# Cross-attention in float32 on one core: the products with the values in batch 6 issued as two runs of two head groups instead of four runs of one

## What is computed

```python
Q = (query @ Wq.T + bq); K = (key_value @ Wk.T + bk); V = (key_value @ Wv.T + bv)
scores = jnp.einsum('bhqd,bhkd->bhqk', Q, K) / np.sqrt(D_K)
attn = jax.nn.softmax(scores, axis=-1)
context = jnp.einsum('bhqk,bhkd->bhqd', attn, V)
output = context @ W_o.T + b_o
x = output + query
return (x - mean(x)) / sqrt(var(x) + 1e-5) * ln_gamma + ln_beta
```

## Time and profile before

| what | before |
|---|---|
| median of 3 runs | 141.59 us (141.34 to 142.11) |
| the profiled execution's own time | 142.33 us |
| its span, first to last instruction | 140.4 us |
| PE busy | 130.2 us, 93% of the span |
| DVE busy | 96.9 us, 69% |
| ACT busy | 88.2 us, 63% |
| POOL busy | 82.2 us, 59% |
| granted TensorE clock, mean | 0.999 |

### The profile page before, as it was taken

One profiled execution on the slowest core, in us unless ns is written; L12 is line 12 of the kernel. 1 busy time (PEld: TensorE's weight loads), 2 busy tenths in 40 slices (PEclk: granted clock), 3 DMA queues, 4 the chain that ended last, 5 costly groups with the idle time before them and its releaser, 6 DMA issues.

```text
span 140.4 us, 3935 instructions
## 1 busy us (share of the span) xinstructions
PE 130.2 (93%) x1481; PEld 115.1 (82%) x1481; DVE 96.9 (69%) x226; ACT 88.2 (63%) x179; POOL 82.2 (59%) x105
## 2 busy tenths in 40 slices
PE   4999989799999999998999999999999999999960
PEld 4899966689788979897999998998989888877730
DVE  5977799888837875678559756975687788521442
ACT  3468544458485847668585859574958556788510
POOL 8357899993722853205079975860489106589181
PEclk9999999999999999999999999999999999999999
DMA  4996797882279832651226025642280000011102
GB/s 98 351 363 231 208 295 226 304 254 108 61 185 298 244 131 69 217 173 55 72 105 229 5 72 170 230 163 60 75 298 3 24 20 5 4 37 35 37 0 65
DMA packets 16067, 19.59 MB, mean 139 GB/s; under 512 B 2592, under 2 KB 15456, under 8 KB 16048
## 3 DMA queue, kind: packets, MB, share of 16 engines
q1 hardware_dynamic: 14944, 17.42, 38.5%
q0 software_dynamic: 640, 1.64, 4.4%
q10 hardware_dynamic: 464, 0.28, 0.7%
HBM read 6.30 MB, written 0.92 MB: 51 GB/s over the span
## 4 chain that ended last, share of the span: by engine, by line
PE 84%; DVE 6%; DMA 5%; issue 1%; ACTq 1%; POOLq 0%; SPq 0%; ACT 0%; DVEq 0%
PE m_bank L885 19%; PE pv_bank L991 14%; PE mx_bank L940 14%; PE st_bank L973 14%; PE m_bank L1022 4%; PE st_bank L885 3%; DMA q_stack<-shift_half 3%; DVE mx L742 3%; PE mx_bank L1071 3%; PE m_bank L1002 2%; PE m_bank L913 2%; PE mx_bank L973 2%; DMA q_stack<-shift 2%; PE m_bank L1010 1%; ACTq L277 1%
## 5 line engine op out<-in xcount | busy, mean ns | idle before, releaser
L742 DVE TENSOR_REDUCE mx<-mx_bank 112x1 f32<-112x375 f32 x128 | 63.8, 540 | 21.8 <-PE mx_bank L940 21.5
L628 ACT ACTIVATE pw<-st_bank 125x448 f32<-125x448 f32 x86 | 45.3, 544 | 19.4 <-PE st_bank L973 18.9
L940 PE MATMUL mx_bank<-k_stack,q_stack 128*112 128x376 f32 x128 | 43.2, 352 | 0.1
L973 PE MATMUL st_bank<-q_stack,k_stack 128*125 128x224 f32 x172 | 34.8, 284 | 1.8 <-DMA q_stack<-shift_half 1.3
L973 PEld LDWEIGHTS st_bank<-q_stack,k_stack 128*125 128x125 f32 x172 | 28.6, 186 | 5.2 <-issue 2.7
L940 PEld LDWEIGHTS mx_bank<-k_stack,q_stack 128*112 128x112 f32 x128 | 22.0, 176 | 2.9 <-issue 1.5
L431 POOL TENSOR_TENSOR k_hl<-k_full,k_hl 128x376 fp32r<-128x376 f32 x10 | 10.3, 1032 | 19.8 <-ACT k_hl L549 19.8
L991 PE MATMUL pv_bank<-pw,v_sb 125*17 125x112 f32 x744 | 21.5, 260 | 0.0
L991 PEld LDWEIGHTS pv_bank<-pw,v_sb 125*17 125x17 f32 x744 | 16.7, 97 | 3.1 <-issue 1.9
L885 PE MATMUL m_bank<-w_hl,c_hl 128*125 128x256 f32 x126 | 18.1, 282 | 0.0
L405 POOL TENSOR_TENSOR c_hl<-c_raw,c_hl 128x752 fp32r<-128x752 f32 x6 | 11.2, 1861 | 10.6 <-ACT c_hl L520 10.6
(11 more groups left out here) (115 smaller groups left out, 177.4 us busy)
## 6 DMA issues: line engine op xcount, KB each, us to landing
k_stack<-k_hl SPq DMA_DIRECT2D x48, 188.0 KB, 2.7
c_raw<-ctxT SPq DMA_DIRECT2D x8, 375.0 KB, 3.9
q_stack<-q_hl SPq DMA_DIRECT2D x9, 112.0 KB, 2.3
x_space<-x_nat SPq DMA_DIRECT2D x4, 224.0 KB, 3.1
out<-yo SPq DMA_DIRECT2D x8, 112.0 KB, 2.0
pw<-wT SPq DMA_DIRECT2D x2, 256.0 KB, 4.7
q_stack<-q_hl POOLq DMA_DIRECT2D x3, 168.0 KB, 2.8
q_stack<-q_hl SPq DMA_DIRECT2D x3, 168.0 KB, 2.9
```

The costliest lines, as they stand in the source:

```text
L628: nc.scalar.activation(p_tile[0:KC, n % PR, :, :], st_of(n)[0:KC, 0:4 * Q].rearrange("p (j q) -> p j q", j=4), ACT.Exp, scale=float(DK) ** ...
L742: nc.vector.tensor_reduce(mx[b % 2][:, h % 2, q_pair(h // 2):q_pair(h // 2) + 1], mx_bank[n % MR][0:Q, 0:KV], axis=AX_X, op=ALU.max, negat ...
L940: nc.tensor.matmul(mx_bank[n % MR][0:Q, 0:KVP], q_stack[k][:, side, q_pair(h // 2), b - Q_STACKS[k][0], :], k_stack[b % 3][:, h // 2, :], ...
L973: last = nc.tensor.matmul(st_of(n)[0:KC, k * 2 * Q:(k + 1) * 2 * Q], k_stack[i % 3][:, 2 * g + k, c * KC:(c + 1) * KC], q_stack[qk][:, :, ...
```

## The change

One constant is different, so that the rule for runs of two groups holds for batch 6 too, up to unit 86:

```diff
         WIDE = UNITS * (B - 2) + 4
         LATE = WIDE + 2
-        SINGLE = UNITS * (B - 2) + NC
+        SINGLE = UNITS * (B - 1) + NC
         wide_ring = st_bank + mx_bank[0:2]
```

## The result

| | before | after |
|---|---|---|
| median of 20 runs each | 141.55 us (141.27 to 142.69) | 142.28 us (141.79 to 143.01) |
| the profiled execution's own time | 142.33 us | 141.97 us |
| its span | 140.4 us | 140.2 us |
| granted TensorE clock, mean | 0.999 | 0.998 |

The ratio is 1.0041, with a 95% interval of 1.0026 to 1.0056: by the ratio the change makes the kernel slower by 0.58 us, with an interval of 0.37 to 0.79 (the medians as they stand in the table are 0.73 apart). The forecast was +0.60.

What follows compares the result with a forecast made beforehand. TensorE (PE), busy 93% of the span, was taken as the bound. Last group's end -0.28, then +0.95 to the copy in place of 0.07, gives +0.60 us: 141.59 + 0.60 = 142.2 us, range 141.5 to 142.8.

Steps and rivals of the forecast that it cites:

- The saving: On PE, merging two runs into others saves 0.33 us each, -0.66 us in all.
- Step 1: Unit 77's pair, no longer covered by group 0's run, waits for unit 75's exponential to free its bank: +0.26 us.
- step 2: PE's projection (0.86), transposes and units 78 and 79, then run one without a wait, ending at 121.56 us.
- Step 3: Unit 84's pair, fifth behind run one, waits for unit 80's exponential to free its bank: +0.33 us.
- the ring: Four banks used in turn by score pairs; unit 84's pair therefore needs unit 80's exponential to end.
- Step 4: Unit 84 also waits for the maxima's DMA, landing about 122.4 us, ahead of the exponential's 122.56: no cost, margin 0.15.
- Step 5: Projection, unit 85's pair, then run two without a wait, ending at 125.50 us; PE 0.28 us ahead of before.
- Step 6: Unit 86's pair follows run two; its exponential precedes the copy of the sums on ACT, ending the copy 0.60 us later.
- Step 7: PE finishes units 87 and 88, stands until the copy; transposes begin 0.60 us later, the whole tail moving with them.
- saving and waits cancel: Rival: the two bank waits cost nothing, the copy is back at 126.39 and nothing moves; 141.6 us, chance 0.15.
- the saving reaches the end: Rival: the full 0.66 us comes through if the copy does not hold the transposes; 141.0 us, chance 0.08.

Runs made afterwards that it cites:

- experiment 8: Changed kernel with unit 86's pair ahead of the second run, batch 5's projection ahead of unit 84, batch 4's ahead of unit 77 (its input copied earlier): ratio 0.9934.
- Experiment 3: Changed kernel with the output projection of batch 5 ahead of unit 84's score pair instead of behind it: ratio 1.0019, stretch 9.40 us.
- experiment 6: Changed kernel with the transpose of batch 7's maxima ahead of the output projection of batch 4: ratio 1.0066, stretch 10.04 us.
- Experiment 4: Kernel before with only the second run merged (groups 2 and 3 behind unit 85): ratio 1.0068; profiled a second time for its stretch, 10.18 us.
- Experiment 1: Changed kernel with unit 86's score pair back ahead of the second run: ratio 1.0001, stretch 9.11 us.
- experiment 2: Changed kernel with ACT's copy of batch 6's sums behind unit 85's exponential instead of unit 86's: ratio 0.9962, stretch 8.88 us.
- experiment 5: Only the first run merged (groups 0 and 1 behind unit 79), groups 2 and 3 apart as in the kernel before: ratio 1.0019, stretch 9.18 us.
- experiment 7: Changed kernel with unit 86's pair ahead of the second run and batch 5's projection ahead of unit 84: ratio 0.9969, stretch 8.81 us.

## Why the prediction was right, step by step

- **The saving, 0.66 us.** Right in size: experiment 8, in which neither bank wait is left and the copy isn't late, has 0.63. It was not enough to foretell the sign. The Trainium skill (TensorEngine Tiling (Array Packing), Key Properties) states that a change of tiling mode drains the array. The trace agrees, with the 0.63.
- **Step 1, the wait at unit 77, 0.26.** Measured 0.25. Missing from the step is the projection behind it, 0.08 longer than the 0.86 of step 2.
- **Step 3, the wait at unit 84, 0.33.** Measured 0.31. Experiment 3 takes it away by cover alone, experiment 6 shows that the ring holds it even with an early DMA.
- **Step 4, the DMA of the maxima, margin 0.15.** The step was wrong in its sum, without an effect on the result. L955 ends at 120.48, where its next piece begins; I had added its 0.10 once more. By the step's own sum it should come 0.64 us earlier, not 0.74. Measured it came 0.57 earlier, the projection's 0.08 being the rest (the first issue is at 119.38 - 116.71 = 2.67 from the transposes of batch 5, before at 120.81 - 117.57 = 3.24), and the margin was nothing: landing and exponential fell on the same 121.75. Experiment 4 shows what lies behind: 0.71 us of idle weight loads, named DMA.
- **Step 5, the second run 0.28 ahead of where the last group had ended.** Counted from L1002 of batch 5 it ends at 124.69 - 116.71 = 7.98, and the last group before at 125.78 - 117.57 = 8.21: 0.23 ahead. The difference is the 0.08, less 0.03 by which the two waits were shorter.
- **Step 6, the copy behind the exponential of unit 86, 0.60 later.** The copy begins at 125.58 - 116.71 = 8.87 where it began at 125.85 - 117.57 = 8.28: 0.59 later. Experiment 1 and experiment 2 undo it from either side, on PE and on ACT, and each takes the loss away. The order of ACT's list is what held the copy; in the changed kernel the sums were ready 0.89 us before it began. The Trainium skill (PSUM — Partial Sum Buffer, Engine vs sequencer instructions) states that this queue is strictly first in, first out. The trace agrees, with the 0.89. That the sum came out within 0.01 is partly luck: the run ends 0.05 later than step 5 has it, and the copy begins 0.44 behind the start of the exponential, not 0.50.
- **Step 7, all behind the transposes moves with them.** The last instruction of the chain (`137.60 0.48 DVE yo L864` before, `137.34 0.48 DVE yo L864` after) starts 137.60 - 126.53 = 11.07 us behind them before, and 137.34 - 126.25 = 11.09 after. Right.
- The rival in which **saving and waits cancel** is what experiment 1 is: with the copy in its place both sums meet (0.66 against 0.25 + 0.08 + 0.31), and the ratio is 1.0001. The rival in which **the saving reaches the end** is experiment 8.

What stays open: that the projection behind unit 77 takes 0.08 more because it waits for its input is inferred from one lag and not tested. The ratios of experiments 2, 5 and 8 are each 0.2 to 0.3 us from what their stretches say (0.9934 is -0.94 us, the stretch -0.63), within their intervals; I can't tell whether more than the scatter of the runs is in it.

## What to carry to other kernels

Merging short runs saves a price for each change of shape on PE (here 0.33 us a run). Before counting on it, look at what each of the small runs covered: a wait on a bank, a copy of the next input, a DMA on its way, and above all which instruction moved to the other side of the run, and what stands behind its consumer in the next engine's list. The saving came through only once the copy was out from behind the late exponential (experiments 2, 7 and 8), and in full once other work covered the waits; the repairs cost nothing but the order of a few lines. When the sum of some waits happens to equal the loss, that is no proof: undo the suspected step with the waits left in.

## What the runs showed that I had not expected

The lead of 0.86 us with which the changed kernel's profiled execution comes to the change arises in its first 28 us, where both kernels have the same lists. 0.28 of it are there by 20.5 us: the first projections (L913) take 2.50 us in its chain and 2.79 in the one before. The other 0.58 come up to the next use of `shift_half` (L747, at 26.86 and 27.72 us): the chain before passes over a DMA, 4.40 us for `q_stack<-shift_half` at 21.07, and the chain after runs on VectorE there and doesn't wait for it. The chains of experiments 3 and 6 and of experiment 4's second execution pass over this DMA too, those of 1, 2, 5, 7 and 8 don't, so it is a matter of the execution. Together this is more than the change costs, which is why two single profiles compared by their spans give the wrong sign.

One execution of the kernel of experiment 4 took 247.47 us, with PE busy 238.4 us in place of 130, at a granted clock that the profile gives as 1.0, the upper level. ACT's exponentials took their usual 544 ns. A granted clock near 1 thus doesn't prove that the work ran at its usual pace; the durations of the matmuls do (a run of 48 records took 2.51 us there in place of 1.27).
